# A graph and memory network on one core: the last row tile's table gathers fetch 98 rows instead of 128

## The reference, cut to what matters

```python
scores, best = lax.top_k(all_scores, TOP_K)
indices = jnp.take_along_axis(all_idx, best, axis=-1)
w_d = w_down[indices]
w_u = w_up[indices]
inner = jnp.einsum('bd,bhkd->bhk', x, w_d)
vals = jax.nn.relu(inner) * jax.nn.softmax(scores, axis=-1)
out = jnp.einsum('bhk,bhkd->bd', vals, w_u)
```

## Time and profile before

| What | Value |
|---|---|
| median of the runs | 2357.53 us (2357.14 to 2363.02) |
| the profiled execution's own time | 2359.55 us |
| its span | 2357.9 us |
| busy: PE, DVE, ACT, POOL | 1991.7, 1408.1, 798.8, 784.0 us |
| gathers at L547 | 640, 651.8 us of POOL |
| products at L607 | 640, 443.5 us of DVE |
| matmuls at L818 | 2560, 467.0 us of PE |
| bytes read from HBM | 452.91 MB |

### The profile page before, as it was taken

How to read it: one execution, slowest core, us unless ns; L and a number is a source line. 1 busy time by engine, 2 the same in 40 slices (tenths; PEclk the granted TensorE clock), 3 DMA queues, 4 the chain that set the end, 5 groups by cost and what they waited for, 6 DMA issues and landing times. The chain is left out here.

```text
span 2357.9 us, 31714 instructions
## 1 busy us (share of the span) xinstructions
PE 1991.7 (84%) x10088; PEld 1140.5 (48%) x10089; DVE 1408.1 (60%) x3985; ACT 798.8 (34%) x1912; POOL 784.0 (33%) x862
## 2 busy tenths in 40 slices
PE   8987888988988988977688978799999875999992
PEld 4334443333333333332145433688888433777771
DVE  4885078988988898898651352677877530000002
ACT  2023133333343343333222220577777211222220
POOL 0000067777777777777400000111110012111113
PEclk9998999989989988989898989899999976999996
DMA  4012189999999999999810460742421133313434
GB/s 149 6 51 111 58 331 395 398 408 407 406 403 403 395 406 404 392 400 397 323 54 0 148 202 21 213 138 91 143 83 56 46 113 128 111 65 110 178 107 139
DMA packets 149322, 494.42 MB, mean 210 GB/s; under 512 B 21428, under 2 KB 22100, under 8 KB 149072
## 3 DMA queue, kind: packets, MB, share of 16 engines
q0 software_dynamic: 100720, 358.29, 39.2%
q1 hardware_dynamic: 48480, 134.63, 17.1%
HBM read 452.91 MB, written 39.94 MB: 209 GB/s over the span
## 5 line engine op out<-in xcount | busy, mean ns | idle before, releaser
L547 POOL DMA_INDIRECT m_ring<-in_table,m_rows_at x640 | 651.8, 1018 | 235.5 <-issue 132.6
L818 PE MATMUL m_acc<-m_ring,m_diag 64*64 64x512 f32 x2560 | 467.0, 695 | 130.7 <-ACT m_diag L718 130.4
L607 DVE CUSTOM_DVE_ANT_0 m_ring<-m_ring,m_coming,m_part 128x512 f32<-128x512 f32 x640 | 443.5, 748 | 47.7 <-DMA m_ring<-in_table,m_rows_at 37.2
L818 PEld LDWEIGHTS m_acc<-m_ring,m_diag 64*64 64x64 f32 x2560 | 151.4, 149 | 414.9 <-ACT m_diag L718 340.8
L718 ACT ACTIVATE m_diag<-m_eye,m_inner 128x64 f32<-128x64 f32 x640 | 222.3, 348 | 309.4 <-DVE m_inner L607 309.4
L1848 PEld LDWEIGHTS e_psU<-e_rowsT,x_w 128*128 128x128 f32 x1472 | 169.7, 194 | 13.4 <-issue 13.4
L1848 PE MATMUL e_psU<-e_rowsT,x_w 128*128 128x128 f32 x1472 | 170.1, 277 | 2.2 <-DVE e_rowsT L1879 1.1
L1358 DVE TENSOR_TENSOR a_pT<-a_psT,a_pT 128x512 fp32r<-128x512 f32 (+1 forms) x240 | 140.0, 598 | 40.4 <-ACT a_pT L1393 36.8
L1857 PE MATMUL e_psY<-x_w,e_hT 128*128 128x512 f32 x368 | 161.7, 592 | 0.0
L1393 ACT ACTIVATE a_pT<-a_psT 128x512 fp32r<-128x512 f32 (+1 forms) x240 | 122.5, 528 | 97.3 <-PE a_psT L1292 97.3
L1292 PE MATMUL a_psT<-ident,a_prob 128*128 128x128 f32 x800 | 118.5, 280 | 28.3 <-ACT a_prob L1387 20.1
(11 more groups left out here) (320 smaller groups left out, 2721.9 us busy)
## 6 DMA issues: line engine op xcount, KB each, us to landing
x_w<-in_we SPq DMA_DIRECT2D x16, 2048.0 KB, 11.0
xnT<-edge_log_counts SPq DMA_DIRECT2D x40, 640.0 KB, 3.9
m_ring<-in_table,m_rows_at POOLq DMA_INDIRECT x640, 7.7
qk_parts<-p_parts SPq DMA_DIRECT2D x32, 320.0 KB, 4.3
a_k<-qk_parts SPq DMA_DIRECT2D x32, 320.0 KB, 9.5
edge_shares<-shareT SPq DMA_DIRECT2D x10, 640.0 KB, 3.0
m_share<-edge_shares SPq DMA_DIRECT2D x10, 640.0 KB, 7.1
edge_log_counts<-p_log_cnt SPq DMA_DIRECT2D x10, 640.0 KB, 6.2
```

Source lines behind the costliest of these rows:

```text
L547: pool.indirect_dma_start(ring[:, slot, :], None, ins["table"], bass.IndirectOffsetOnAxis(rows_at[:, h, k:k + 1], 0)).then_inc(s_land[slot ...
L607: dve.tensor_tensor_reduce(ring[:, slot, 0:D], ring[:, slot, 0:D], coming[:, t % 2, :], part[:, b, k:k + 1], 0.0, ALU.mult, ALU.add, inner ...
L818: mm = pe.matmul(acc[to, i, :], diag[rows, h % 2 * TOPK + k, :], ring[rows, nth % RING, D:2 * D], start=h == 0 and k < 2, stop=h == HEADS ...
```

## The change

The gathers of the last tile name 98 partitions of the slot and 98 indices, those of the other tiles 128 as before. The products and matmuls over the slot keep all 128 partitions, so in the last tile the last 30 partitions of a slot hold what the tile before left there.

```diff
                         if nth >= RING:
                             pool.wait_ge(s["slot_free"], nth - RING + 1)
-                        pool.indirect_dma_start(ring[:, slot, :], None, ins["table"],
-                                                bass.IndirectOffsetOnAxis(rows_at[:, h, k:k + 1], 0)).then_inc(s_land[slot], 16)
+                        r = rows_of(t)
+                        pool.indirect_dma_start(ring[0:r, slot, :], None, ins["table"],
+                                                bass.IndirectOffsetOnAxis(rows_at[0:r, h, k:k + 1], 0)).then_inc(s_land[slot], 16)
```

## The result

The changed kernel is slower: 2389.63 us (2387.7 to 2393.22, 4 runs) against 2357.34 us (2355.46 to 2363.02, 4 runs), a ratio of 1.0131 with a 95% interval of 1.0114 to 1.0148. That is 32 us, outside the range of 2351.0 to 2361.5 and on the other side than forecast.

The account below looks back on a forecast made before the run. The prediction took POOL's issuing of gathers as the bound, transfers nearly as slow. Landing 1.4 us plus POOL's pace 1.1 us made 2.5 us off the median of 2357.53, forecast 2355.0 us, range 2351.0 to 2361.5.

Parts of the forecast that it names:

- the last landing: End of the last tile: the last gather's product starts 4.37 us after it, not 5.73; 1.36 us won, taken as 1.4.
- What sets the pace in the kernel before: Last tile: POOL, issuing gathers 1.32 us apart, sets the pace; the transfers at 1.30 us are nearly as slow.
- The sum of 2.5 us: Whole change: 1.4 us from the last gather's landing plus 1.1 from POOL's pace, 2.5 us earlier.
- POOL's time does not hang on the queue: Last tile's gathers: POOL's own durations need nothing from the DMA queue; fewer rows or bytes shorten them by 0.
- The landing that relief would give: Last tile: with the queue emptied, the last gather's product starts 4.37 us after it instead of 5.73.
- POOL's phase against VectorE: Last 20 intervals: earlier landings shift products against gathers, 1.25 us each instead of 1.314; 1.3 us, of which 1.1 counted.
- the rival of a bad phase: Last 20 intervals: shorter lag lets a 1.65 us interval hold itself; 5.7 us slower, 2363.2 us; chance 0.12.
- The evidence from L1911: Two 98-row gathers of half the bytes land after 4.3 and 4.4 us, 128-row ones before them 5.2 in the middle.
- The Trainium skill's rule on 14 engines: Last tile's transfers: 98 partitions go on 14 engines, 7 rows each; the sum 0.1 us less than with an even share.
- The Trainium skill's rule for 128 partitions: Transfers: for bandwidth use 128 partitions; cited as speaking against 98, given no size.
- the unmoved landing: Last tile: rows stay on their engines, some keep 8 rows and their queue; 2357.5 us, at best 0.3 less; chance 0.15.
- The slower rival: Same as the rival of a bad phase: POOL's last 20 intervals at 1.65 us, 5.7 us slower; chance 0.12.

## Why the prediction was wrong

**The step that failed** is in the part on the last landing: "With 98 rows a transfer takes 98/128 of 1.30 us = 1.00 us, 0.30 less". It took 1.75 us by the rate of 230 GB/s, 1.77 by the products. I scaled the time with the bytes and held the rate of 402 GB/s fixed. But that rate belongs to the 128-row form. The sum ends there: with 1.75 us the transfers are slower than POOL (1.32 us), the queue fills instead of emptying, the landing becomes 22 us instead of 4.37, and every later step follows the transfers.

What the runs show of the cause, with 64 rows: the rate hangs on the receiving partitions, in groups of four, of which the ones 32 apart share something; by the packets' times, two engines at it at once go at half speed each. There the prediction of this picture held to the factor (0.32 against 0.16 us for the middle packet, and a landing that moved by 2.2 us for a step of four partitions). The Trainium skill describes it ("SBUF — State Buffer", Door 1: The DMA port swizzle): 16 ports, each with the partitions p to p + 3 and those 32 further on, 0 to 63 reaching only eight of them. The trace agrees, 208 GB/s at 0 to 63. In the 128-row transfer, by the Trainium skill ("DMA: Bandwidth & Descriptors", The descriptor swizzle), each engine writes one port. No run here shows which engine wrote which rows.

By that port map of the Trainium skill, 98 rows from partition 0 on leave the fullest port with 8 rows to take, no fewer than 128 rows do. So the number of ports alone would allow 1.3 us, and not the 1.00 us of the prediction (an estimate from the map): even a transfer without collisions would have won nothing.

Why 98 rows took 1.75 us and not 1.3 is argued, not shown. My reading is that the one-to-one match is lost: shares of 7 consecutive rows cross the groups, and an engine whose port is taken waits with all its later rows behind it. Two things keep it open. Where two engines met in the runs with 64 rows, a packet took 0.32 us, and 0.16 otherwise; with 98 rows the middle half of the packets lies from 0.26 to 0.31 us, with 96 rows from 0.24 to 0.26, and of either none is under 0.17. And worked through as a rule (each engine takes its share in order, one row at a time at a port, 0.163 us a row) it gives, as an estimate, anything from 150 to 380 GB/s for 98, 120 and 126 rows, by which waiting engine goes first and which engines sit out, and no run shows either; for 96 and 112 rows it gives some 270 to 330, over the measured 265 and 251. So the rule makes a rate under 402 GB/s plausible, and does not give the measured ones. No kernel placed 98 rows, or any count but 64, elsewhere than from partition 0 on.

What the runs do show is a regularity. The time of a gather is its bytes by the rate from 1110 to 1150 us, and the number of rows on one engine is read from the packets (last section):

| Rows in the gather | rows on one engine | us a gather | us for a row of the share |
|---|---|---|---|
| 128 | 8 | 1.32 | 0.17 |
| 126 | 9 | 2.15 | 0.24 |
| 120 | 8 | 1.94 | 0.24 |
| 112 | 7 | 1.83 | 0.26 |
| 98 | 7 | 1.75 | 0.25 |
| 96 | 6 | 1.48 | 0.25 |

For the five counts below 128 in this table a gather took 0.24 to 0.26 us for each row of an engine's share (64 rows at 0 to 63, 4 to an engine, took 0.31). In this order 98 rows, 7 to an engine, come next to 112, and 126 rows, 9 to an engine, are the slowest. Why it is 0.25 us a row and not 0.16 stays open.

**The rest, point by point.**

- *What sets the pace in the kernel before*: right for the kernel before, as far as the runs reach. With 7.7 MB instead of 15.8 in 40 us (64 rows at 32 to 95) the next stage starts at 1165.06, 0.7 us sooner; at 34, at 0 and at 36, 2.0, 1.8 and 2.8 us sooner. The sum of 2.5 us was of that size. It is no test of it, since one trace each doesn't tell such differences apart and POOL's own time is shorter with 64 rows (872 ns at least, against 932). What it missed is that POOL stood before the transfers by only 0.02 us in a gather (1.32 against 1.30), so that there was nothing to absorb an error in the transfer's time.
- *POOL's time does not hang on the queue*: right. In the changed kernel gathers land 22.7 us after issue and still take 0.95 us in the middle.
- *The landing that relief would give*: 4.37 us for 98 rows was not tested as such. For 64 rows, 4 to an engine, the same working gives 0.95 + 3.56 - 4 x 0.16 = 3.9 us; free of collisions 3.7 were measured.
- *POOL's phase against VectorE*: seen both ways. At 0 to 63 the last 21 intervals are 1.23 us on average (from 1124.09 to 1149.89), at 32 to 95, with the earliest landing of all, 1.38 (from 1125.02 to 1153.97). So a shorter landing can come with a slower POOL, as the rival of a bad phase has it, though not with its 1.65 us. Which of the two kernels gained more is not shown: the next stage starts 0.7 us sooner at 32 to 95 and 1.8 at 0 to 63, but counted from each tile's own first gather (1071.13 and 1069.03 us, 1069.54 before) it is 2.3 and 1.3 us sooner.
- *The evidence from L1911* was misread. Two gathers of half the bytes, with little behind them, landed early, where 64 gathers of 98 rows one behind the other took 22.7 us in the middle. A landing at low load says nothing of a rate.
- *The Trainium skill's rule on 14 engines* was taken only for its rows on each engine (7, not 8); the packets agree with it (last section). The Trainium skill's rule for 128 partitions, which spoke against the change, was the one to price: as a rate between half and all of 402 GB/s it would have given, as an estimate, 98 rows 1.0 to 2.0 us, and a high end of about 2357.5 + 64 x 0.7 = 2402.
- *The rivals*: the unmoved landing supposed that the engines keep their rows; under it the transfers could not have become slower, and they did. The slower rival had the right sign and the wrong mechanism: its 5.7 us were to come from gathers of over 1.3 us in a row on POOL, and these stayed at 0.95 in the middle.

No version that is faster than the kernel before and computes the same came out of this. Every form with at least 98 rows other than 128 was slower.

## What to carry to other kernels

Fewer rows in a gather are not less transfer time: cutting 128 partitions to 98 made each row 1.8 times as slow, 112 and 126 made it 1.6 and 1.7 times as slow. Where gathers are back to back and the DMA engines are always in use, keep all 128 partitions, padding included, or use a run of partitions that meets each group of four and its partner 32 further on only once (32 to 95; tried here with 64 rows alone, and with POOL setting the pace). And before bytes are taken off a queue that is full, look how far the engine ahead of it is from being the limit: at 1.32 against 1.30 us there was next to nothing to win, and 32 us were lost.

## What the runs showed beyond that

- A count that 16 does not divide brings more small packets (4 B): 16 a gather with 64, 96, 112 and 128 rows, 24 with 120 (490 for 20.6), 30 with 98 and 34 with 126 (633 for 18.6). Together with the rows these are 80, 112, 128 and 144 packets a gather, and 144, 128 and 160, in each case 16 x (rows on one engine + 1), if 98 and 126 rows go to 14 engines (7 and 9 each) and 120 to 15 (8 each). So the packets read as if every engine gets the same number, and an engine without rows gets a small one in place of each. 126 rows decide it: spread over 16 engines, 8 at most to each, they would need no more than 144 packets. The small packets are not the main cost (112 rows have 16 and are slow).
- POOL's time for a gather does hang on the count a little, though not in its order: its shortest in the last tile was 872 to 887 ns with 64 rows, 898 with 96 and 910 with 112, but 932 with 98, 967 with 120, 958 with 126 and 933 with 128.
- A gather on POOL that starts while VectorE's product over the ring runs ends a fixed time after that product: 0.81 us in the kernel before (44 of the last tile's 64 gathers start so), 0.75 us with 64 rows at 32 to 95 (44 again). With nothing changed but the receiving partitions, the pace of POOL moved between 1.23 and 1.38 us; that these waits account for all of it is not shown.
